# Every eighth batch's values gathered twice instead of put aside, and tile-number loads spread behind the additions, in a graph network on one core

## The reference

```
Q = (enh @ Wq + bq)...; K = ...; V = ...           # enh = layernorm(x) + 0.1 * query_emb
mod_k  = K[src] + 0.2 * rel_w[type]
scores = einsum('ehd,ehd->eh', Q[dst], mod_k) / D ** 0.5
ex     = exp(scores - segment_max(scores, dst)[dst])
agg    = segment_sum((ex / segment_sum(ex, dst)[dst]) * V[src], dst)
```

## Time and profile before

| | us |
|---|---|
| median of 3 runs | 5515.21 (5502.7 to 5521.81) |
| the profiled execution's own time | 5508.83 |
| its span | 5507.0 |
| score phase, first to last score | 190 to 747 |
| attend phase, first hits to last addition | 806 to 1236 |

### The profile page before, as it was taken

The page is one execution under the profiler, slowest core; times in us unless marked ns, Lnnn a source line. Parts: engine busy times, 40 slices in busy tenths (PEclk is TensorE's granted clock), DMA queues, the critical chain, the costliest instruction groups (busy, mean ns, idle before and its releaser), DMA issues. The chain is left out here.

```text
span 5507.0 us, 68392 instructions
## 1 busy us (share of the span) xinstructions
PE 4188.6 (76%) x19994; PEld 3157.8 (57%) x19994; DVE 2366.0 (43%) x4715; ACT 1183.2 (21%) x2721; POOL 2134.7 (39%) x2064
## 2 busy tenths in 40 slices
PE   5899955654745776899976999766569999665689
PEld 2566634433643554799976888444447677444455
DVE  4688885557335444366555000322223222222253
ACT  1233320001221000223322444200004333000032
POOL 0577745445256776000010111377750000577710
PEclk9899978886778999999986999568889999778788
DMA  2699954321563333110012999233340000233300
GB/s 75 219 286 287 296 173 130 127 84 45 155 196 104 103 103 102 72 35 7 7 57 78 335 323 307 72 101 102 103 120 1 1 1 15 84 103 103 97 20 15
DMA packets 375626, 639.13 MB, mean 116 GB/s; under 512 B 73045, under 2 KB 269816, under 8 KB 375168
## 3 DMA queue, kind: packets, MB, share of 16 engines
q1 hardware_dynamic: 275006, 342.72, 18.9%
q0 software_dynamic: 100288, 292.14, 18.0%
HBM read 526.12 MB, written 108.57 MB: 115 GB/s over the span
## 5 line engine op out<-in xcount | busy, mean ns | idle before, releaser
L2451 POOL DMA_INDIRECT gathered_rows<-k_table,index x1176 | 1155.8, 983 | 1073.4 <-ACT index L2440 716.0
L2537 PE MATMUL sum_ps<-gathered_rows,hit 128*125 (+1 forms) x3328 | 984.7, 451 | 661.7 <-SPq L2457 430.6
L2537 PEld LDWEIGHTS sum_ps<-gathered_rows,hit 128*125 128x125 f32 (+1 forms) x3328 | 703.3, 221 | 942.8 <-issue 827.4
L96 POOL DMA_INDIRECT rows_all<-kv_table,src_of_visit x416 | 436.6, 1049 | 221.9 <-issue 111.8
L2521 DVE TENSOR_TENSOR node_sums<-node_sums,sum_ps 125x256 f32 x244 | 102.8, 421 | 770.6 <-PE sum_ps L2537 770.6
L1045 PE MATMUL ps_sum<-summand,hit 128*125 128x261 f32 x832 | 259.7, 465 | 180.6 <-DVE odd_sums L1006 162.3
L2440 ACT ACTIVATE index<-src_of_chunk 128x4 int32<-128x4 int32 x294 | 59.2, 205 | 1417.2 <-DMA gathered_rows<-k_table,index 1382.1
L1045 PEld LDWEIGHTS ps_sum<-summand,hit 128*125 128x125 f32 x832 | 176.1, 222 | 264.1 <-issue 232.3
L776 PE MATMUL ps_q<-q,hit_t 125*128 x832 | 294.8, 437 | 22.4 <-issue 20.6
L993 POOL TENSOR_TENSOR summand<-v_rows,scores 128x1024 f32<-128x1024 f32 x104 | 213.2, 2052 | 208.5 <-PE ps_sum L1045 198.3
L2745 PE MATMUL qk_ps<-window_sums,composed 128*128 128x126 f32 (+1 forms) x2400 | 292.1, 279 | 0.0
(11 more groups left out here) (483 smaller groups left out, 6735.4 us busy)
## 6 DMA issues: line engine op xcount, KB each, us to landing
w<-in_L_ffn_W SPq DMA_DIRECT2D x112, 1024.0 KB
v_kept<-rows_all SPq DMA_DIRECT2D x104, 512.0 KB, 5.0
v_rows<-v_kept SPq DMA_DIRECT2D x104, 512.0 KB, 3.6
gathered_rows<-k_table,index POOLq DMA_INDIRECT x1176, 2.7
w<-in_L_ffn_w SPq DMA_DIRECT2D x64, 256.0 KB, 3.8
b<-in_L_ffn_b SPq DMA_DIRECT2D x88, 128.0 KB, 4.6
y_slots<-y SPq DMA_DIRECT2D x32, 256.0 KB, 4.6
y_slots<-y SPq DMA_DIRECT2D x56, 128.0 KB
```

What stands on the lines that cost most here:

```text
L96: pool.indirect_dma_start(env.ring[:, k % KEPT_RING, i, :], None, env.kv_table, bass.IndirectOffsetOnAxis(env.src_of_visit[:, k * VB + i:k ...
L2451: pool.indirect_dma_start(self.rows[:, (q % SLOTS) * CHUNKS + c, :], None, self.table, bass.IndirectOffsetOnAxis(self.index[:, q % SLOTS, ...
L2537: mm = pe.matmul(sum_ps[0:rows, k % banks, 0:D], hit[:, g % (lead + 1), i * chunks + c, :], gather.rows[:, ds(first[i] + c, 1), :].rearran ...
```

## The change

A batch with k % 8 == 7 is no longer "kept". In the score phase its gathers fetch only the key half of each row (`kv_halves` is `kv_table` seen as 6,250 rows of 1 KB, and the key half of node n is row 2n), and SP does not store it. In the attend phase SP does not load it; instead POOL, ahead of the multiplication of batch k with k % 8 == 0, issues four gathers that fetch the value halves (row 2n + 1) of batch k + 7. The row numbers 2n and 2n + 1 are made once, by two DVE instructions in `qkv_phase`. Thirteen of the 104 batches are of that kind. Beside it, each tile number of the next batch is now loaded right behind one addition, where all four were loaded behind the last one.

```
+AGAIN = 8
+def is_kept(k):
+    return k % AGAIN != AGAIN - 1
+def kept_in_place(k):
+    return sum(is_kept(j) for j in range(k % KEPT_RING, k, KEPT_RING))

 def start_gather(env, pool, k):
     for i in range(VB):
+        if is_kept(k):
+            pool.indirect_dma_start(env.ring[:, k % KEPT_RING, i, :], None, env.kv_table, index)...
+        else:
+            index = bass.IndirectOffsetOnAxis(env.half_row[:, 0, k * VB + i:k * VB + i + 1], 0)
+            pool.indirect_dma_start(env.ring[:, k % KEPT_RING, i, 0:D], None, env.kv_halves, index)...

 class Gather:
-            pool.wait_ge(self.kept[k % KEPT_RING], 16 * (k // KEPT_RING))
+            pool.wait_ge(self.kept[k % KEPT_RING], 16 * kept_in_place(k))
 ...
         for k in range(self.batches):
+            if not is_kept(k):
+                continue
             self.wait(sp, k)
             sp.dma_start(self.env.v_kept[k], ...)

 qkv_phase, DVE, ahead of the additions of the queries:
+                for part in range(2):
+                    v.tensor_scalar(env.half_row[:, part], env.src_of_visit[:], 2, part, ALU.mult, ALU.add)

 attend_phase, POOL:
                 for k in range(batches):
                     slot = k % SLOTS
-                    pool.wait_ge(landed[k % deep], 16 * (k // deep + 1))
+                    if k % deep == 0 and k + last < batches:
+                        if k > 0:
+                            pool.wait_ge(weighed, k)
+                        for i in range(VB):
+                            pool.indirect_dma_start(rows[:, last, i, :], None, env.kv_halves, bass.IndirectOffsetOnAxis(
+                                env.half_row[:, 1, (k + last) * VB + i:(k + last) * VB + i + 1], 0)).then_inc(env.gathered[last], 16)
+                    if is_kept(k):
+                        pool.wait_ge(landed[k % deep], 16 * (k // deep + 1))
+                    else:
+                        pool.wait_ge(env.gathered[last], base + 16 * VB * (k // deep + 1))

 attend_phase, DVE:
                     for i in range(VB):
                         if k * VB + i >= 2:
                             v.wait_ge(summed, k * VB + i - 1)
                         v.tensor_tensor(here, here, ps_sum[0:P, k % 2, i, 0:VC], ALU.add).then_inc(summed, 1)
+                        if k + 1 < batches:
+                            following.append(tile_of(k + 1, i))
-                    add(k, tiles)
-                    if k + 1 < batches:
-                        tiles = tiles_of_batch(v, env.tile_of_visit, k + 1, T)
+                    tiles = add(k, tiles)
```

More of the change, by code:

```diff
@@ L95, in start_gather @@
     for i in range(VB):
-        pool.indirect_dma_start(env.ring[:, k % KEPT_RING, i, :], None, env.kv_table, bass.IndirectOffsetOnAxis(
-            env.src_of_visit[:, k * VB + i:k * VB + i + 1], 0)).then_inc(env.gathered[k % KEPT_RING], 16)
+        index = bass.IndirectOffsetOnAxis(env.src_of_visit[:, k * VB + i:k * VB + i + 1], 0)
+        if is_kept(k):
+            pool.indirect_dma_start(env.ring[:, k % KEPT_RING, i, :], None, env.kv_table, index).then_inc(env.gathered[k % KEPT_RING], 16)
+        else:
+            index = bass.IndirectOffsetOnAxis(env.half_row[:, 0, k * VB + i:k * VB + i + 1], 0)
+            pool.indirect_dma_start(env.ring[:, k % KEPT_RING, i, 0:D], None, env.kv_halves, index).then_inc(env.gathered[k % KEPT_RING], 16)
 class Gather:
@@ L125, in sync @@
         for s in range(KEPT_RING):
-            sp.wait_ge(self.kept[s], 16 * len(range(s, self.batches, KEPT_RING)))
+            sp.wait_ge(self.kept[s], 16 * sum(is_kept(k) for k in range(s, self.batches, KEPT_RING)))
     def wait(self, engine, k):
@@ L963, in attend_phase @@
     batches = VT // VB
-    deep = 8
+    deep = AGAIN
     with ExitStack() as st:
@@ L972, in attend_phase @@
         cleared, hits_made, multiplied, summed, weighed, copied = [ph.sem() for _ in range(6)]
-        landed = [ph.sem() for _ in range(deep)]
+        landed = [ph.sem() for _ in range(deep - 1)]
+        last = deep - 1
+        base = env.gathered_base[last]
+        env.gathered_base[last] += 16 * VB * len(range(last, batches, deep))
         with nc.Block() as block:
@@ L999, in _, with tile_of @@
             def _(v):
+                def tile_of(k, i):
+                    return v.value_load(env.tile_of_visit[0:1, k * VB + i:k * VB + i + 1], min_val=0, max_val=T - 1)
                 def add(k, tiles):
+                    following = []
                     for i in range(VB):
@@ L1006, in add @@
                         v.tensor_tensor(here, here, ps_sum[0:P, k % 2, i, 0:VC], ALU.add).then_inc(summed, 1)
+                        if k + 1 < batches:
+                            following.append(tile_of(k + 1, i))
+                    return following
                 def hits(k):
@@ L1015, in _ @@
                     hits(k)
-                tiles = tiles_of_batch(v, env.tile_of_visit, 0, T)
+                tiles = [tile_of(0, i) for i in range(VB)]
                 for k in range(batches):
@@ L3325, in build @@
         env.kv_table = nc.dram_tensor("kv_table", (N, 2 * D), F32).ap()
+        env.kv_halves = env.kv_table.rearrange("n (two d) -> (n two) d", two=2)
         env.v_kept = nc.dram_tensor("v_kept", (VT // VB, 128, VB, D), F32).ap()
@@ L3335, in build @@
         env.src_of_visit = sb(env, x_stack, "src_of_visit", [128, VT_PAD], I32)
+        env.half_row = sb(env, x_stack, "half_row", [128, 2, VT_PAD], I32)
         env.rel_dst = sb(env, x_stack, "rel_dst", [128, VT_PAD])
```

## The result

| | before | changed |
|---|---|---|
| median of 15 runs each, us | 5515.21 (5496.15 to 5521.81) | 5490.29 (5481.02 to 5503.59) |
| ratio, 95% interval | | 0.996 [0.995, 0.997] |
| profiled execution, its span, us | 5508.83, 5507.0 | 5493.03, 5491.0 |

The change makes the kernel 25 us faster. The forecast said 48, so the sign was right and the size twice too large. (The numbers of single phases come from one profiled execution of each kernel.)

What follows compares the result with a forecast made beforehand. PE was taken to set the score phase's pace and DVE's queue, loading four tile numbers a batch, the attend phase's. 103 - 23 - 18 - 17 + 3 = 48 us gained gave 5467 us on the runs' scale, range 5420 to 5498.

Steps and rivals of the forecast that it cites:

- The loads: Attend phase: tile-number loads run under DVE's additions, period falls from 4.00 to 3.0 us, 103 us gained.
- R5: Rival, 5%: each interleaved load waits for the addition ahead, period stays near 4.0, time within 0.3%.
- (a): Attend phase: PE at half clock needs 3.75 us a batch, no longer hidden; takes back 23 us.
- (b): Attend phase: DVE's hits meet POOL's multiplications and are held up in every second batch; takes back 18 us.
- (c): Attend phase: second gathers on POOL delay the start and prolong batches after each round; takes back 17 us.
- (d): Score phase: 13 stores and 13 half gathers fewer; 3 us gained.
- R2: Rival, 5%: transfers bound the score phase after all; 46 us more gained, 5419 us.
- (e): Setup: two DVE instructions making row numbers, at most 1.4 us, covered by POOL's gathers; cost nothing.
- R3: Rival, 13%: the path moves to PE and POOL more than counted; gain 10 to 25 us, about 5498 us.
- R1: Rival, 12%: the loads win nearly all, (a) and (b) near zero; about 5425 us.
- R4: Rival, 5%: hits caught behind POOL's multiplication every batch while the queue cannot load; period 4.74 us, 5590 us.
- the signs named: Attend phase: period 3.0 to 3.1 us, issue idle near 0.6 or gone, phase some 380 us; wrong if hits' mean passes 1.8.

Runs made afterwards that it cites:

- Number 1: Kernel before with only the tile-number loads moved behind each addition, no batch gathered twice; ratio 0.9873.
- number 9: Changed kernel with a fill of 8 columns and a wait for it behind each round of four gathers; ratio 0.9899.
- number 5: Kernel before with the loads moved, and four fills of an unused tile on POOL ahead of batch 0 of each eight; ratio 0.9884.
- Number 4: Kernel before with only the score phase's edit; in the attend phase SP loads the preceding batch's stored values instead of second gathers; ratio 1.0003.
- 7: Changed kernel with the attend phase's hits made on ACT instead of DVE, gathers kept; ratio 0.9831.
- 8: Kernel before with the loads moved and the attend phase's hits made on ACT, nothing gathered twice; ratio 0.9816, 5419.24 us.
- number 10: Kernel before with the loads moved, and one unused gather then a 3,100-column fill on POOL ahead of batch 0 of each eight; ratio 0.9908.
- number 3: Changed kernel with the four second gathers issued one at a time, ahead of batches 0, 1, 3 and 5 of each eight; ratio 0.9875.
- number 6: Changed kernel with the four second gathers issued in two pairs, ahead of batches 0 and 4 of each eight; ratio 0.9911.

## Why the prediction was half right

**The loads: right.** Forecast 103 us, from a period of 4.00 down to 3.0. The undisturbed period is 3.07 to 3.09, so 103 x 0.92 = 95 us. The reading of the earlier trace rows, that a queue loads while its engine computes, holds, and R5 with it falls.

**(a) and (b), PE's clock and the ordinary meetings: right in kind, too large.** They were put at 41 us. Number 1 has both and no gathers: its hits come 3.214 us apart in the mean, (3.214 - 3.09) x 103 = 13 us (16 from the 3.25 between additions). The clock was 0.99, so (a) was near its lower bound of 0; the mean of 0.84 came from the loop that was to go. As for (b), nearly every hits instruction, not every second one, takes over 1 us (median 1.20), but the queue loads numbers meanwhile, and little of it stays on the path. The Trainium skill ("SBUF — State Buffer", section "Who interferes with whom"), cited in (b), says that the one that comes second is blocked until the other's instruction ends; the hits of up to 2.4 us agree with that, but its full price, 63 us, was not paid.

**(c), the gathers: the step that failed.** It said: "Two batches of such a round at 4.0 instead of 3.0 [...] 1 us x 12 = 12", and with the start, 17 us in all. Number 1 against the changed kernel gives 394.8 - 335.5 = 59 us between the first and last additions, and with the start, from the first hits, 411.8 - 345.3 = 66. One batch of each round takes about 7.7 us, not two 4.0. The step had the scene right, POOL catching up back to back, and assumed that the hits would get in between two multiplications as in the earlier trace rows. No row of the trace of before could show otherwise: it has no gather in a stage in which DVE makes hits beside multiplications of POOL.

The whole price lies in the long periods: twelve of 8.27 us between additions, 12 x (8.27 - 3.25) = 60 us, while the other 91 have a mean of 3.24, as in number 1. So the lower clock of the changed kernel's stretch, 0.88 against 0.99, adds nothing to the others. The 59 us divide by number 9: 394.8 - 357.7 = 37 us go to the keeping-out that a stop ends, 357.7 - 335.5 = 22 to POOL's lateness with ordinary meetings in its wake. That is 22 against 12 for the same part of the forecast, so even the ordinary part was low; number 5, at 352.3, gives 17. (Two batches of 1 us in twelve rounds are 24; the forecast took off half for what (b) counts, without working it out.)

The start came near by luck: the first addition comes 7 us later behind the first hits (17.0 us against 9.8), where 5 were put. Half of that is the later first multiplication, which was forecast; the other half is the hits of 6.01 us. With the stop of number 9 the first addition comes 3.6 us later.

The reckoning in the forecast's terms for the attend phase, from the first hits to the last addition: 95 - 13 - 66 = 16, and 429.2 - 411.8 = 17 measured. The other 8 of the 25 us lie outside the phase. About 3.5 of them may belong to the setup, which ended that much earlier in each kernel with the table of row numbers; why was not followed. The rest is within what phases differ by themselves.

The price of the gathers has a loose end too: it is 66 us in this phase of two profiled executions, on two chips, and 45 to 51 in the medians of whole runs. Part of the difference stands behind the phase: that code, the same in all kernels, took 4531 to 4541 us in the five executions with the score phase's edit on the other two chips and 4549 and 4553 in the two without (4256 to 4265 against 4266 to 4274 on the chip of 5516 us and in the comparison of the change). Number 4, which has that edit too, gained nothing as a whole, so what sets this is open, and the size of (c) is known to some 20 us only. At either size it is far above the 17 forecast.

**(d), the score phase: right as far as can be told.** 3 us forecast, 0 measured (number 4; its interval runs from 8 us faster to 11 slower). R2, which expected 46 us from the transfers, is refuted, and so is the reading that the phase became slower.

**(e), the row numbers: right.** Two instructions of together 0.67 us, at 135.7 us, inside their cover.

**The rivals.** The result lies in the band of R3, 5498 being named and 5490 measured, but not for R3's reason: PE's clock and the ordinary meetings, whose bounds it used, cost less than forecast, not more. That the measured time lies inside the stated range at all is luck in this sense: two misses, (a) and (b) 28 us too high and (c) 49 too low, made up for each other in part. R1, the loads winning nearly all, is what numbers 1, 7 and 8 show when the gathers are gone or harmless. R4 named the lock, but not how it costs. The hits were caught in nearly every batch of number 1, as it asked, and its other condition, a queue that cannot load while they stand, was false. What cost was one stand in eight batches through three multiplications. Of the signs named, the issue idle went, the period came to 3.09; but the hits' mean of 1.62 us, under the limit of 1.8 that was set, already told the story through its maximum of 6.0, which no sign asked for. The attend phase of 412 us instead of 380 was the plain miss.

## What to carry to other kernels

Loads of register values placed between an engine's instructions run under them; here that is worth 0.92 us in each of 103 batches. When work is added to POOL ahead of multiplications that DVE's two-input instructions must wait for, count not only its duration but in what run of instructions it stands: issue gathers one at a time, put a short stop behind them, or move DVE's two-input instruction to ACT. And a half of a change is best tried alone: the loads alone gained nearly three times as much as both together.

## What the runs showed of the hardware

**A gather changes who gets in.** Behind an indirect DMA of POOL, multiplications back to back kept a waiting DVE instruction with two SBUF inputs out for two or three of them, up to 6.4 us (4.70 us even with a fill of 2.7 us between); behind fills, or after a stop of 0.1 us, it got in behind the first, at 2.4 us at most. The multiplications also run closer when they keep it out: three took 5.61 to 5.62 us, against 6.07 when the hits got in between. The rule of the Trainium skill named above ends at one instruction; it does not cover this case. What in the engine a gather sets and a stop clears, no run here shows.

**A gather held nobody, but for the last one ahead of multiplications.** Hits that began beside a gather which a further gather or a fill followed took 0.68 to 0.72 us, as at 1002.50 of the changed kernel; so did those beside a fill, at 1091.56 of number 10. But beside the last gather ahead of multiplications the multiplication won even where the hits began first: 0.55 us ahead of it they stood 4.87 us (at 949.56 of number 3), 0.23 ahead 6.40 (at 827.68 of number 6). Without a gather, hits that began 0.11 us ahead kept their 0.69, and the multiplication took 2.34. A gather that starts beside hits lasts longer: 1.13 us in the median in the changed kernel and 1.26 in number 3, against 0.95.

**ACT was not held.** The hits made on ACT beside the same multiplications took 384 to 389 ns in 416 of 416 cases, and 721 to 724 ns in 104 of 104. The same section of the Trainium skill says that ACT never waits on others' SBUF accesses, and the trace agrees.

**A held engine's queue goes on.** While the hits of 1005.59 stood for 5.87 us, DVE's queue loaded two more numbers, at 1005.76 and 1006.53, and the next three additions came 0.33 us apart instead of up to 0.76. That is why ordinary meetings cost so little of what they show as busy time.
